# An attention and mixture-of-experts kernel on one core: the fp16 upper part of gelu is written by ScalarE instead of VectorE

## What is computed

```python
topk_vals, topk_idx = jax.lax.top_k(xf @ wr + br, 2)
gates = jax.nn.softmax(topk_vals, axis=-1)
h = gelu(einsum('nd,edh->enh', xf, w1) + b1)          # erf form, 1024 hidden units
y = einsum('enh,ehd->end', h, w2) + b2
out = einsum('nk,nkd->nd', gates, y_sel - c_sel + c_sum)
```

## Time and profile before

| | |
|---|---|
| median of 3 runs | 1062.55 us (1061.18 to 1064.93) |
| the profiled execution, its own time | 1066.83 us |
| its span in the trace | 1065.1 us |
| mean granted PE clock | 0.958 of full speed |
| busy over the span: PE, DVE, ACT, POOL | 929.2, 835.0, 495.6, 430.5 us |

### The profile page before, as it was taken

One profiled execution on the slowest core, in us unless ns is written; L12 is line 12 of the kernel. 1 busy time (PEld: TensorE's weight loads), 2 busy tenths in 40 slices (PEclk: granted clock), 3 DMA queues, 4 the chain that ended last, 5 costly groups with the idle time before them and its releaser, 6 DMA issues.

```text
span 1065.1 us, 26698 instructions
## 1 busy us (share of the span) xinstructions
PE 929.2 (87%) x8002; PEld 676.0 (63%) x8003; DVE 835.0 (78%) x2990; ACT 495.6 (47%) x1045; POOL 430.5 (40%) x376
## 2 busy tenths in 40 slices
PE   3688999997989989998896799899999999999920
PEld 1244656555656566565664577788889778988920
DVE  4637789797898988988987789887777887777737
ACT  3256554553555635555355545343444333333304
POOL 6418055383453653735537512223222442322321
PEclk8789999999999999999999989999999999999975
DMA  4785103224133032230133432223223332232356
GB/s 141 250 213 147 32 22 105 80 70 118 35 91 92 25 120 59 62 119 2 51 111 120 159 110 41 41 52 47 46 42 61 81 59 45 50 50 50 50 124 222
DMA packets 61535, 90.33 MB, mean 85 GB/s; under 512 B 8620, under 2 KB 51136, under 8 KB 60384
## 3 DMA queue, kind: packets, MB, share of 16 engines
q1 hardware_dynamic: 45832, 62.73, 19.9%
q0 software_dynamic: 14304, 21.90, 11.2%
q10 hardware_dynamic: 1280, 4.19, 1.1%
HBM read 52.80 MB, written 35.86 MB: 83 GB/s over the span
## 4 chain that ended last, share of the span: by engine, by line
PE 55%; DVE 25%; issue 6%; DMA 6%; SPq 4%; ACT 2%; DVEq 1%; POOL 0%; ACTq 0%; POOLq 0%
PE sm L1375 6%; PE st L1375 5%; PE ms L1160 5%; PE sm L1388 5%; PE pv L1388 5%; PE sm L1242 5%; PE st L1202 4%; PE pv L1222 4%; DVE junk L1780 4%; PE ms L1300 3%; DVE arena_b L1942 3%; DVE arena_b L1940 2%; PE ms L1272 2%; DVE beaten L1727 2%; PE st L1204 2%
## 5 line engine op out<-in xcount | busy, mean ns | idle before, releaser
L1780 DVE CUSTOM_DVE_ANT_0 junk<-sm,mask_ts 128x512 bf16<-128x512 f32 (+3 forms) x512 | 220.1, 485 | 61.1 <-PE sm L1242 58.7
L900 POOL DMA_INDIRECT sums<-arena_b x70 | 112.6, 1609 | 294.7 <-DVE arena_b L1968 280.6
L1028 ACT ACTIVATE arena_b<-st 128x512 f32<-128x512 f32 x320 | 180.2, 598 | 101.6 <-PE st L1204 100.2
L1202 PE MATMUL st<-arena_a 128*128 128x384 f16 (+3 forms) x512 | 126.5, 304 | 24.1 <-ACT arena_b L1028 16.7
L1242 PE MATMUL sm<-arena_a 128*128 128x512 f16 (+3 forms) x512 | 112.9, 309 | 18.0 <-DVE maxes L1780 11.9
L1942 DVE TENSOR_TENSOR arena_b<-arena_b 128x256 f16<-128x256 f32 x280 | 120.2, 429 | 9.6
L1099 ACT ACTIVATE arena_b<-sm,arena_b 128x256 f32<-128x256 f32 x140 | 66.1, 474 | 125.5 <-PE sm L1375 107.0
L1375 PE MATMUL st<-arena_b,arena_a 128*128 128x256 f16 x840 | 115.6, 275 | 7.7 <-DVE arena_b L1659 6.9
L1940 DVE CAST arena_b<-arena_b 128x256 f16<-128x256 f32 x280 | 88.8, 317 | 38.5 <-ACT arena_b L1099 36.9
L1388 PE MATMUL pv<-arena_a,arena_b 128*128 x864 | 118.0, 275 | 0.0
L1099 ACT ACTIVATE arena_b<-st,arena_b 128x256 f32<-128x256 f32 x140 | 65.9, 473 | 111.0 <-PE st L1375 95.9
(11 more groups left out here) (292 smaller groups left out, 1675.0 us busy)
## 6 DMA issues: line engine op xcount, KB each, us to landing
arena_b<-slots SPq DMA_DIRECT2D x37, 260.0 KB, 2.8
arena_a<-w SPq DMA_DIRECT2D x8, 1024.0 KB, 6.8
arena_b<-x_tr SPq DMA_DIRECT2D x8, 512.0 KB, 4.2
q_rows<-arena_b SPq DMA_DIRECT2D x32, 128.0 KB
k_rows<-arena_b SPq DMA_DIRECT2D x32, 128.0 KB
arena_a<-q_rows SPq DMA_DIRECT2D x32, 128.0 KB
arena_a<-k_rows SPq DMA_DIRECT2D x32, 128.0 KB
res<-x_tok POOLq DMA_DIRECT2D x8, 512.0 KB, 4.7
```

The costliest lines, as they stand in the source:

```text
L900: pool.indirect_dma_start(sums, bass.IndirectOffsetOnAxis(ap=token_now[:, 1 - par, m:m + 1], axis=0), y_out[1 - par][:, m, :], None, compu ...
L1028: act.activation(probs[:, q, :], st_ps[piece % 2][:, :], ACT.Exp, scale=SCORE_SCALE).then_inc(exp_done, 1)
L1202: pe.matmul(out[:, at:at + width], ks[:, h % 2, h // 2, s * P:(s + 1) * P], qs[:, h // 2, s * P:T], start=m == 0, stop=False, skip_group_c ...
L1780: last = dve.tensor_tensor_reduce(junk[:, n % 3, at:at + width], sm_ps[n % 3][:, at:at + width], mask_ts[:, T - width:T], 1.0, NEG, ALU.ad ...
```

## The change

ACT runs the same gelu a second time from the same bank, with an fp16 output straight into `g_hi`. DVE's cast goes. PE's wait for a free bank and DVE's wait for the old bias now count `ghi_done`, since the second gelu reads both the bank and the bias. Before the first chunk's second write ACT waits for `y_ready`, as DVE did, so that `g_hi` isn't overwritten while PE still reads it. It holds for all 35 tiles.

```diff
                         act.activation(g_32[:, hc % 4, :], u_bank(hc)[:, 0:ROWS], ACT.Gelu, bias=b1_now[:, par, hc:hc + 1],
                                        scale=1.0 / W_SCALE).then_inc(gelu_done, 1)
+                        if hc == 0 and later(t, 2):
+                            act.wait_ge(y_ready, n_of(t - 1))
+                        act.activation(g_hi[par][:, hc, :], u_bank(hc)[:, 0:ROWS], ACT.Gelu, bias=b1_now[:, par, hc:hc + 1],
+                                       scale=1.0 / W_SCALE).then_inc(ghi_done, 1)
                         if hc == 4:
                             rows_high(t + 1, 1 - par)
...
                     if hc >= 4 or later(t, 1):
-                        pe.wait_ge(gelu_done, n_of(HC * t + hc - 3))
+                        pe.wait_ge(ghi_done, n_of(HC * t + hc - 3))
...
                 if later(t, 2):
-                    dve.wait_ge(gelu_done, n_of(HC * (t - 1)))
+                    dve.wait_ge(ghi_done, n_of(HC * (t - 1)))
...
                         dve.wait_ge(gelu_done, n_of(HC * t + hc + 1))
-                        dve.tensor_copy(g_hi[par][:, hc, :], g_32[:, hc % 4, :]).then_inc(ghi_done, 1)
                         dve.wait_ge(ghi_done, n_of(HC * t + hc + 1))
                         dve.tensor_tensor(g_lo[par][:, hc, :], g_32[:, hc % 4, :], g_hi[par][:, hc, :], ALU.subtract).then_inc(hid_done, 1)
```

## The result

| | before | after |
|---|---|---|
| median | 1063.03 us (20 runs) | 1059.17 us (1050.98 to 1064.17, 20 runs) |
| span of the profiled execution | 1065.1 us | 1059.4 us |
| ratio, with 95% interval | | 0.9952 (0.9936 to 0.9968) |
| mean granted clock | 0.958 | 0.954 |

The change is worth 3.9 us by these medians. The lines of code moved by four behind the edit, and by three behind the removed cast: PE's first and second layer are L1379 and L1392, the transposes L1142, DVE's subtraction L1945, `rows_low` L1663, the gates L1929 to L1937, the output L1965 and L1971; ACT's second gelu is L1103.

What follows compares the result with a forecast made beforehand. DVE was taken as the bound in tiles 0 to 6, PE from 880 to 1015 us. Gains of 1.1 + 3.7 + 3.5 + 2.8 = 11.1 took 1066.83 to 1055.7, less 4.3 for the median: 1051.5 us, range 1044.5 to 1059.

Steps and rivals of the forecast that it cites:

- Term A: Tile 0: without the casts DVE gets to `rows_low` sooner despite POOL's exclusive port lock, shortening PE's 5.16 us wait; -1.1 us.
- term B: Tiles 1 to 5: PE's pauses for `rows_low` and row loads shrink as DVE loses eight casts a tile; -3.7 us.
- Term C: Tile 6: DVE's lag goes, and with it PE's 2.37 us pause before a transpose and its slow restart; -3.5 us.
- the pause at z of tile 7: A small PE pause in tile 7, put at 0.5 us of gain and counted by the prediction within tiles 7 to 22.
- Term D: Tiles 7 to 22: row loads issued earlier cut PE's load waits, with 0.5 us for z in tile 7; -2.8 us.
- the loop: The twelve loop tiles: the second gelu fits, so a tile stays at 10.92 us; change 0.
- these bursts: Weight remainders on DVE, 2.35 us for two, clustered in tile 1 and from the end of tile 2 into tile 3.
- rival 1: Loads stay late because `added` or ACT's weight chunks take DVE's place; gain 4.0 us, time 1058.5 us, chance 0.19.
- 5.2 less 1.4: Tiles 1 to 5: 5.2 us of pauses with their restart costs, of which 1.4 us was expected to be left.
- Carrying the 4.3 us: The profiled execution stood 4.3 us above the runs' median; the forecast took the same offset from 1055.7 to 1051.4 us.
- Rival 4: Slower, 1069 us: a later `g_hi` delays gates, load and transposes in 32 tiles where PE barely pauses; chance 0.05.
- Rival 2: Nearly all of PE's idle time goes, with pause and clock costs, 20.7 us in all; time 1042 us, chance 0.10.

Runs made afterwards that it cites:

- a kernel with still less between DVE's operations: The kernel before with neither ACT nor DVE writing `g_hi`, which is zeroed once while PE still runs its products: 1055.93 us, ratio 0.9914.
- four buffers: The changed kernel with four instead of two `token_now` buffers in the unrolled tiles: 1047.72 us, ratio 0.9858; repeated on a slower chip: 1098.71 us, ratio 0.9887.
- three gelus: The changed kernel with a third gelu per chunk into a buffer that nobody reads: 1061.77 us, ratio 0.9977.

## Why the prediction was wrong, point by point

By its own terms, from the lengths of the same tiles in the two profiles (tiles 1 to 5 of the first profile hold the half clock):

| term | forecast | measured | changed kernel again |
|---|---|---|---|
| A, tile 0 | -1.1 | -2.7 | -2.5 |
| B, tiles 1 to 5 | -3.7 | +1.0 | -2.1 |
| C, tile 6, with the pause at z of tile 7 | -4.0 | -4.5 | -4.3 |
| D, tiles 7 to 22 without z | -2.3 | -1.5 | -2.4 |
| the loop | 0 | +1.1 | +0.7 |
| sum | -11.1 | -6.6 | -10.6 |

The attention part ended 1.3 us later in the profile after, which the change doesn't touch, and a little was lost at the end: the spans differ by 5.7. The last column is the profile of the changed kernel again, from another chip. Its sum lies near the forecast, and so do the two later medians (10.0 and 10.6 us below the kernel before), but partly by luck: A won 1.4 us more than forecast and B 1.6 less, with the slow issue in place.

**The step that failed is term B**: "its load issues are on time in three of five tiles, and late by 0.35 and 0.7 us in the tiles behind these bursts". The prediction followed DVE with its own durations and gave the scatter-add, on which DVE's gates wait, no time at all. The load for the transposes in tile 4 was issued at 652.56, and PE stood ready at 652.10: with 2.76 us to land it was 3.2 late, not 0.7. The casts had broken DVE's run, as each subtraction waited for the cast ahead of it (0.04 us apart in the earlier trace rows). Without them POOL's issue stretched to 5.4 us. That is the wait of rival 1, `added`, in the place it named, but by a mechanism that it didn't name: it expected an add no slower than before. That its time, 1058.5, is within 1 us of the median is luck, since it kept half of C's pause, which went, and priced no half clock. Own waits between subtractions (1.76), a gap of 0.35 us (2.77) and a kernel with still less between DVE's operations (5.37 twice) bear the mechanism out. What the slow issue costs by itself no run isolates; with four buffers, where wait and slow issue are both gone, the expert part is 6.8 us shorter.

The half clock behind the new pause is the rest of B: 2.8 us in tile 4 in one profile, nothing in the other. Without it B would be -1.8. (By its own parts, 5.2 less 1.4, B comes to 3.8, not 3.7; nothing hangs on it.) C counted on the clock when a pause goes, B didn't when one comes.

**Term A** was right in its mechanism, the exclusive lock: a subtraction that met POOL stood until POOL's 2.40 us operation ended. The pause shrank by 1.85 where 1.1 was forecast, as DVE got more through between POOL's operations, and 0.8 more came from a shorter stretch at half clock behind it, which I had left as it was. The Trainium skill, "SBUF — State Buffer", section "SBUF: two separate sides", states this lock, and the trace agrees. The box on DMAs issued from GpSimd in that section also says that GpSimd can't write their descriptors while DVE holds the shared ports; it speaks of DVE's two-port performance modes. Here the issue was held by subtractions and weight remainders with two SBUF inputs, and not by `rows_low`, which has one (the 5.38 us issue). The prediction had weighed the lock for POOL's arithmetic alone.

**Term C** held: DVE's lag went, the pause of 2.37 with it, and its slow restart. **Term D** was too high for the first profile: four waits of 0.4 to 2.1 us stay, one of them behind eight scatters of the last batch that POOL had queued before its add. In the profile of the changed kernel again D held. **The loop** was right in its 10.92 us, and lost 1.1 us in its first two tiles (11.72 and 11.24). A pause of 0.64 is in it, for a load that was issued 3.87 us ahead like the others and took 4.5 to land; the rest, 0.3, wasn't followed. **Carrying the 4.3 us** over to the median added to the miss: the changed kernel's profiled execution took 1061.11 us, 1.9 above its median, so 2.3 of the 7.7 us between forecast and median come from there. Medians of the changed kernel spread as much between chips (0.9952 and 0.9918).

Rival 4 fell: but for the first two no loop tile grew, not even with three gelus. Rival 2's 1042 was out of reach by the lock alone, though four buffers came to 1047.72.

## What to carry to other kernels

When work leaves DVE, look at what used to slip into the gaps that now close: POOL's issue of a DMA took three times as long here once DVE's operations with two SBUF inputs followed each other without one. Where a wait guards a tiny buffer (16 bytes a partition here), give it more buffers together with the change that makes it critical; tried alone, before, it shows nothing. And price a pause with the clock behind it, as a thing that happens in some executions and not in others: 3.6 us of 1050 hung on it here.

## What the runs showed of the hardware that was not expected

- POOL's issue of the first half of an indirect DMA took 1.55 to 2.1 us with DVE idle or with gaps between its operations, 2.77 (five profiles) and 3.90 (one) where a gap of 0.2 to 0.35 us came later in the run, and 5.37 to 5.38 (four profiles) where none came. From the 1.63 of the kernel before to the 5.38 it ended 1.43 to 1.45 us after the last DVE operation ahead of the gap, or ahead of `rows_low`, which reads PSUM. Second halves under DVE's operations took 2.1 to 2.5 us, also under runs without a gap; what lets them in is open.
- A pause of 3.15 us of TensorE was followed by full clock, one of 3.22 at the same place by half clock; pauses of 2.08 and 2.13 likewise. Nothing read in these profiles tells the cases apart, and it stays open.
- One chip ran the same kernel in 1111 us and the others in 1062 to 1064. The difference lies in the attention part and in waits marked "issue"; its cause wasn't tested.
